# A selective scan rebuilt: one scan instruction for two states, decays in two places, D x as a matmul, B and C loaded in eight pieces

## What is computed

```python
x_inner, z = split(x @ W_in.T)
x_conv = silu(depthwise_causal_conv(x_inner, w_conv, b_conv))       # 4 taps
delta, Bm, Cm = split(x_conv @ W_x.T, [1024, 1040])
delta = softplus(delta @ W_dt.T + b_dt)
A = -exp(A_log)
decay = exp(d_t[..., None] * A)                                     # for each row t
state = decay * state + B_t[:, None, :] * x_t[..., None]            # 16 states a channel
y_t = einsum('bds,bs->bd', state, C_t) + x_t * D
out = (y * silu(z)) @ W_out.T                                       # added to x
```

## Time and profile before

| | us |
|---|---|
| median of 3 runs | 2681.13 (2676.42 to 2688.78) |
| the profiled execution, its time | 2680.24 |
| its span on the core | 2678.3 |
| first scan to last gate | 511.68 to 761.5 |
| busy in the whole span: TensorE, VectorE, ScalarE, GpSimd | 2498.9, 1819.6, 1121.8, 598.3 |

### The profile page before, as it was taken

The page is one execution under the profiler, slowest core; times in us unless marked ns, Lnnn a source line. Parts: engine busy times, 40 slices in busy tenths (PEclk is TensorE's granted clock), DMA queues, the critical chain, the costliest instruction groups (busy, mean ns, idle before and its releaser), DMA issues.

```text
span 2678.3 us, 33407 instructions
## 1 busy us (share of the span) xinstructions
PE 2498.9 (93%) x11618; PEld 1680.4 (63%) x11618; DVE 1819.6 (68%) x1995; ACT 1121.8 (42%) x1360; POOL 598.3 (22%) x420
## 2 busy tenths in 40 slices
PE   6999988887866999999999999999898899999998
PEld 5778767644333777777655555555486677777775
DVE  5878854388989577778875666666435766666665
ACT  2334422365444322222245555555333444555543
POOL 4555544388852311111200000000000000000000
PEclk9999999999977999999999999999898899999999
DMA  7677755622111233433332331332111366666563
GB/s 275 227 243 259 259 155 185 223 69 74 37 63 47 110 144 133 180 125 144 140 111 95 102 111 49 112 101 95 63 61 79 116 217 235 232 223 222 220 221 138
DMA packets 123660, 394.71 MB, mean 147 GB/s; under 512 B 23664, under 2 KB 39228, under 8 KB 97072
## 3 DMA queue, kind: packets, MB, share of 16 engines
q1 hardware_dynamic: 95584, 326.82, 34.5%
q10 hardware_dynamic: 27984, 66.66, 7.1%
HBM read 304.14 MB, written 89.30 MB: 147 GB/s over the span
## 4 chain that ended last, share of the span: by engine, by line
PE 72%; DVE 10%; DMA 9%; POOL 3%; ACT 3%; issue 2%; ACTq 1%; SPq 0%; DVEq 0%; POOLq 0%
PE ps L2079 16%; PE ps L2080 15%; PE ps L2081 15%; PE ps L2458 10%; PE ps L2468 9%; DMA w_halves<-unit_lo 7%; PE ps L2365 3%; DVE ps L1612 3%; POOL work L928 1%; PE ps L2719 1%; DVE work L1615 1%; DMA wT_lo<-w_halves 1%; DVE work L1612 1%; ACTq L1069 1%; DMA x_res<-in_x 1%
## 5 line engine op out<-in xcount | busy, mean ns | idle before, releaser
L1832 DVE TENSOR_TENSOR sums<-sums,pT 128x1024 f32<-128x1024 f32 x272 | 319.0, 1221 | 194.1 <-ACT pT L1313 192.8
L1770 DVE SCALAR_TENSOR_TENSOR peak<-ps,rs_all,peak 128x1024 f32<-128x1024 f32 x272 | 335.6, 1277 | 93.9 <-PE ps L2365 93.7
L1313 ACT ACTIVATE pT<-ps,rs_all 128x1024 f32<-128x1024 f32 x272 | 284.8, 1111 | 230.8 <-PE ps L2458 185.2
L2468 PE MATMUL ps<-pT,values 128*64 128x512 f32 x1088 | 256.4, 602 | 0.0
L2196 PE MATMUL ps<-work,ident 128*128 128x512 f32 x256 | 136.0, 632 | 41.2 <-POOL work L909 26.9
L978 POOL TENSOR_TENSOR cT_lo<-cT_raw,cT_hi 128x512 fp32r<-128x512 f32 x60 | 77.6, 1294 | 352.0 <-ACT cT_hi L1262 352.0
L2468 PEld LDWEIGHTS ps<-pT,values 128*64 128x64 f32 x1088 | 68.8, 136 | 132.9 <-issue 112.0
L1966 DVE TENSOR_TENSOR rgu_lo<-rgu_raw,rgu_hi 128x2048 fp32r<-128x2048 f32 x64 | 143.9, 2288 | 5.1 <-ACT rgu_hi L1396 5.1
L1612 DVE TENSOR_TENSOR_SCAN ps<-ps,work 128x512 f32<-128x512 f32 x97 | 118.3, 1220 | 23.7 <-ACT ps L1185 20.5
L872 POOL TENSOR_TENSOR ctx_lo<-ctx_raw,ctx_hi 128x512 fp32r<-128x512 f32 x64 | 104.3, 1629 | 131.4 <-DVE ctx_hi L1519 131.4
L1185 ACT ACTIVATE ps<-delta,a_neg 128x512 f32<-128x512 f32 x128 | 87.2, 689 | 96.5 <-DVE work L1615 86.6
(11 more groups left out here) (461 smaller groups left out, 6452.9 us busy)
## 6 DMA issues: line engine op xcount, KB each, us to landing
rgu_raw<-in_r_gate_up SPq DMA_DIRECT2D x64, 1024.0 KB, 4.8
rd_raw<-in_r_down SPq DMA_DIRECT2D x32, 1024.0 KB, 4.8
sh_raw<-in_s_parts SPq DMA_DIRECT2D x32, 768.0 KB, 4.3
key_rows<-key_hi SPq DMA_DIRECT2D x17, 1024.0 KB, 3.9
key_rows<-key_lo SPq DMA_DIRECT2D x17, 1024.0 KB, 5.9
value_rows<-values SPq DMA_DIRECT2D x17, 1024.0 KB, 8.9
ctxT_raw<-in_ctx_T SPq DMA_DIRECT2D x16, 1024.0 KB, 6.9
ctx_raw<-in_ctx SPq DMA_DIRECT2D x16, 1024.0 KB, 8.5
```

Source lines behind the costliest of these rows:

```text
L1313: nc.scalar.activation(pT[:, i], ps[:, b:b + 2], ACT.Exp, scale=rs_all[:, bass.ds(c * KT + attend_tile(j, i)[1], 1)]).then_inc(s4_exp.sem, 1)
L1770: nc.vector.scalar_tensor_tensor(peak[:, p], ps[:, b:b + 2], rs_all[:, bass.ds(c * KT + kt, 1)], peak[:, p], ALU.mult, ALU.max).then_inc(s ...
L1832: nc.vector.tensor_tensor(sums[:, p], sums[:, p], pT[:, i], ALU.add).then_inc(s4_sum.sem, 1)
L2468: done = nc.tensor.matmul(ps[e * DK:(e + 1) * DK, 6 + p], values[:, s, kt, h * DK:(h + 1) * DK], pT[:, i, e], start=start and kt == 0, sto ...
```

## The change

`far` steps become 14 whole steps: in these the product of both states is GpSimd's, in the other 50 it is VectorE's. One scan instruction runs over both states (1024 elements); so that nothing passes from one state to the next, the first element of each delta row is 1e22 and the rates are kept at or below -1e-20, which makes the first decay exp of at most -100. The decays get two places (banks 2, 3 and 6, 7), and ScalarE waits for step n - 2. D x is a row formed by ScalarE (`skip_part`) that TensorE adds to the sum; all blocks are summed in bank 0, gates come after step 8k. Relu of block 0 is VectorE's; a small Exp stands after the B and C loads. The sixteen rows of B and of C come in eight DMAs of 1 MB: four of the first half at wx blocks 1 to 4, four of the second after block 7; VectorE waits for the second half at step 4 alone. Six blocks of W_out get places of their own and are loaded after the last dt unit. Three of the four tiles of a block are projected at steps 38 to 41, 44, 52 and 60, the fourth tile (bank 2, a place of decays) at step 62 and behind the loop. `wkv_raw` is loaded when the projection is done, between the two halves of w_q.

```diff
-def far(n):
-    return n % 2 == 1 and n != STEPS - 1
+FAR_STEPS = (3, 8, 13, 18, 23, 28, 33, 37, 41, 45, 49, 53, 57, 60)
+def far(n):
+    return n in FAR_STEPS
+def decay_bank(n):
+    return 6 if n % 2 else 2
+OUT_BANK = (4, 5, 1, 2)
+FIRST_DECAY = 1e22
+LEAST_RATE = -1e-20
...
-PARTS_STEP = {1: 1, 2: 6, **{k: 11 + 4 * (k - 3) for k in range(3, IB)}}
+PARTS_STEP = {1: 1, 2: 5, **{k: 11 + 4 * (k - 3) for k in range(3, IB)}}
-GATES_STEP = {8: (3,), 35: (4, 5, 6, 7)}
+GATES_STEP = {8: (3,), 30: (4,), 33: (5, 6), 36: (7,)}
 def out_rows(n):
-    first = (LATE_PRODUCTS - LATE_AHEAD) // 2
-    if first <= n < first + IB:
-        return (n - first) // 2, (n - first) % 2
-    if n >= 5 * SGS + 4 and n % SGS in (4, 5):
-        return n // SGS - 1, n % SGS - 4
+    if 38 <= n < 42:
+        return n - 38
+    if n >= 5 * SGS + 4 and n % SGS == 4:
+        return n // SGS - 1
```

On SyncE:

```diff
+            sp.wait_ge(stream_mm, streamed("dt", IB - 1))
             for ib in range(IB):
-                if ib < 2:
-                    sp.wait_ge(stream_mm, STREAM_UNITS - 1 + ib)
-                else:
-                    sp.wait_ge(y_out, ib - 1)
-                load_halves(STREAM_UNITS + ib, ib % 2, wo_loaded[ib % 2])
-                if ib == 1:
-                    sp.dma_start(wkv_raw[:], a["L1_xattn_Wkv"].rearrange("(t p) n -> p t n", p=P)).then_inc(w4_loaded[1].sem, 16)
+                if ib == IB - 2:
+                    sp.wait_ge(stream_mm, STREAM_UNITS)
+                for half, halves in enumerate(out_weights(ib)):
+                    sp.dma_start(halves.bitcast(F32), split_dram[STREAM_UNITS + ib, half]).then_inc(wo_loaded[ib // (IB - 2)], 16)
...
             for w in range(2):
+                if w == 1:
+                    sp.wait_ge(s2_out, TT)
+                    sp.dma_start(wkv_raw[:], a["L1_xattn_Wkv"].rearrange("(t p) n -> p t n", p=P)).then_inc(w4_loaded[1].sem, 16)
                 for c in range(W_CHUNKS):
```

On GpSimd:

```diff
+            nc.gpsimd.memset(delta[:, :, 0:1], FIRST_DECAY).then_inc(first_decay, 1)
             def read_far(n):
-                pool.wait_ge(sc_scan, (n + 1) * SG)
-                nc.gpsimd.tensor_tensor(work[:, n % RING, SG - 1], work[:, n % RING, SG - 1], c_row(n % SGS * SG + SG - 1), ALU.mult).then_inc(sc_far, 1)
+                pool.wait_ge(sc_scan, n + 1)
+                nc.gpsimd.tensor_tensor(work[:, n % RING], work[:, n % RING], c_rows(n % SGS), ALU.mult).then_inc(sc_far, 1)
```

On ScalarE:

```diff
+            def load_bc(half, rows, r, k):
+                act_e.dma_start(rows[:, k, NS // 4 * r:NS // 4 * (r + 1)].rearrange("p s t -> p (s t)"),
+                                bc_parts[half, r, k].partition_broadcast(P)).then_inc(bc_loaded[half], 16)
             for ob in range(IB):
...
                 if ob == 1:
                     act_e.wait_ge(bc_stored, 16)
-                    load_bc(0, bc_first)
-            load_bc(1, bc_rest)
+                if 1 <= ob < 5:
+                    load_bc(0, bc_first, (ob - 1) // 2, (ob - 1) % 2)
+            for r in range(2):
+                for k in range(2):
+                    load_bc(1, bc_rest, r, k)
+            nc.scalar.activation(silu_warm[:], neg_half[:, 0:1], ACT.Exp)
...
+                nc.scalar.activation(delta[:, k, 1:T], ps[:, bank, 1:T], ACT.Abs, bias=b_dt[:, k:k + 1]).then_inc(dt_abs, 1)
                 if k:
                     act_e.wait_ge(dt_ready, k)
+                    nc.scalar.activation(bc_rows[:, 1:T], ps[:, bank, 1:T], ACT.Relu, bias=b_dt[:, k:k + 1]).then_inc(dt_relu, 1)
...
+            def skip_part(ib):
+                if ib:
+                    act_e.wait_ge(y_done, ib)
+                nc.scalar.activation(skip_row[:], x_conv[:, ib], ACT.Copy, scale=skip[:, ib:ib + 1]).then_inc(y_skip, 1)
...
+                if n >= 2 and far(n - 2):
+                    act_e.wait_ge(sc_scan, n - 1)
+                elif n >= 2:
+                    act_e.wait_ge(sc_read, near_steps(n - 2))
                 for e in range(SG):
-                    if n and e and far(n - 1):
-                        act_e.wait_ge(sc_scan, n * SG)
-                    elif n:
-                        act_e.wait_ge(sc_read, near_reads(n - 1, e))
-                    nc.scalar.activation(ps[:, DECAY_BANK + e], delta[:, ib], ACT.Exp, scale=a_neg[:, ib, g * SG + e:g * SG + e + 1]).then_inc(sc_decay, 1)
+                    nc.scalar.activation(ps[:, decay_bank(n) + e], delta[:, ib], ACT.Exp, scale=a_neg[:, ib, g * SG + e:g * SG + e + 1]).then_inc(sc_decay, 1)
+                if g == 4:
+                    skip_part(ib)
```

On VectorE:

```diff
-            nc.vector.tensor_scalar(a_neg[:], a_neg[:], -1.0, None, ALU.mult).then_inc(a_ready, 1)
+            nc.vector.tensor_scalar(a_neg[:], a_neg[:], -1.0, LEAST_RATE, ALU.mult, ALU.min).then_inc(a_ready, 1)
...
+            nc.vector.tensor_scalar(bc_rows[:, 1:T], ps[:, STREAM_BANK["dt", 0], 1:T], b_dt[:, 0:1], 0.0, ALU.add, ALU.max).then_inc(dt_relu, 1)
...
             def gate_rows(ib):
-                nc.vector.scalar_tensor_tensor(ps[:, ib % 2], x_conv[:, ib], skip[:, ib:ib + 1], ps[:, ib % 2], ALU.mult, ALU.add).then_inc(y_sum, 1)
-                nc.vector.tensor_tensor(x_conv[:, ib], ps[:, ib % 2], gate(ib), ALU.mult).then_inc(y_gate, 1)
+                nc.vector.tensor_tensor(x_conv[:, ib], ps[:, 0], gate(ib), ALU.mult).then_inc(y_gate, 1)
...
+                dve.wait_ge(sc_decay, (n + 1) * SG)
+                drive, state = flat(work[:, n % RING]), flat(ps[:, decay_bank(n):decay_bank(n) + SG])
+                nc.vector.tensor_tensor_scan(drive if far(n) else state, state, drive, 0.0, ALU.mult, ALU.add).then_inc(sc_scan, 1)
+                if not far(n):
+                    dve.wait_ge(sc_scan, n + 1)
+                    nc.vector.tensor_tensor(drive, state, flat(c_rows(g)), ALU.mult).then_inc(sc_read, 1)
+                if ib and g == 0:
+                    gate_rows(ib - 1)
```

On TensorE:

```diff
             def accumulate(n):
-                if g == 0 and ib >= 2:
-                    pe.wait_ge(y_gate, ib - 1)
+                if g == 0 and ib:
+                    pe.wait_ge(y_gate, ib)
...
                 for e in range(SG):
+                    done = nc.tensor.matmul(ps[:, 0], ident[:], work[:, n % RING, e], start=g == 0 and e == 0, stop=False)
                 done.then_inc(sc_y, 1)
+                if g == SGS - 1:
+                    pe.wait_ge(y_skip, ib + 1)
+                    nc.tensor.matmul(ps[:, 0], ident[:], skip_row[:], start=False, stop=True).then_inc(y_done, 1)
...
+                    for tt in range(TT - 1):
+                        project_rows(ib, tt)
+                if n == STEPS - 2:
+                    pe.wait_ge(sc_read, near_steps(n))
+                    for ib in range(3):
+                        project_rows(ib, TT - 1)
+            for ib in range(3, IB - 1):
+                project_rows(ib, TT - 1)
+            rows_loaded(IB - 1)
+            for tt in range(TT):
+                project_rows(IB - 1, tt)
```

More of the change, by code:

```diff
@@ L33, with near_steps, far_steps @@
 RING = 5
+FAR_STEPS = (3, 8, 13, 18, 23, 28, 33, 37, 41, 45, 49, 53, 57, 60)
 def far(n):
-    return n % 2 == 1 and n != STEPS - 1
-def near_reads(n, e):
-    return sum(SG - far(i) for i in range(n)) + e + 1
-def far_reads(n):
+    return n in FAR_STEPS
+def near_steps(n):
+    return sum(not far(i) for i in range(n + 1))
+def far_steps(n):
     return sum(far(i) for i in range(n + 1))
+def decay_bank(n):
[3 more added lines that the diff above has]
+LEAST_RATE = -1e-20
 EARLY_UNITS = ([("x", n, 0) for n in range(IB)] + [("z", n, 0) for n in range(3)] + [("bc", 0, h) for h in range(2)]
@@ L322, in b_rows, with out_weights, c_rows, flat @@
             return (bc_rest if half else bc_first)[:, 0, n:n + SG]
-        def c_row(n):
-            half, n = divmod(n, NS // 2)
-            return (bc_rest if half else bc_first)[:, 1, n]
+        def out_weights(ib):
+            if ib < IB - 2:
+                return wo_hi[:, ib], wo_lo[:, ib]
+            return tuple(half[:, ib - (IB - 2)].rearrange("p k i -> p (k i)") for half in (wT_hi, wT_lo))
+        def c_rows(g):
+            half, n = divmod(g * SG, NS // 2)
+            return (bc_rest if half else bc_first)[:, 1, n:n + SG]
+        def flat(rows):
+            return rows.rearrange("p b n -> p (b n)")
         s3 = Map(nc, base, 229344)
@@ L915, in add_soft @@
             def add_soft(k):
-                pool.wait_ge(dt_taken, 2 * (k + 1))
+                pool.wait_ge(dt_relu, k + 1)
                 pool.wait_ge(dt_l, k + 1)
-                nc.gpsimd.tensor_tensor(delta[:, k], bc_rows[:], delta[:, k], ALU.add).then_inc(dt_ready, 1)
+                nc.gpsimd.tensor_tensor(delta[:, k, 1:T], bc_rows[:, 1:T], delta[:, k, 1:T], ALU.add).then_inc(dt_ready, 1)
             for n in range(STEPS):
@@ L1605, in _ @@
+            dve.wait_ge(bc_loaded[0], 64)
             for n in range(STEPS):
                 ib, g = divmod(n, SGS)
+                if n == SGS // 2:
+                    dve.wait_ge(bc_loaded[1], 64)
```

(27 more changed lines are left out.)

97 lines of the change are left out of this document (41 added, 56 removed).

## The result

The changed kernel takes 2661.78 us (median of 7 runs, 2655.75 to 2665.54) against 2681.13 (7 runs, 2676.42 to 2688.78): ratio 0.9926, 95% interval [0.991, 0.9942]. The forecast was 2642 and its range ended at 2659: the direction was right, the size was not. 19.4 us were gained where 39 were expected. The profiled execution after has a span of 2659.6 us and TensorE's granted clock at 0.97.

The account below looks back on a forecast made before the run. VectorE was taken to set the scan's length (busy 224.5 of 249.8 us), GpSimd following closely. 2680.24 - 29.3 - 2.5 - 5.9 - 0.8 = 2641.7, with 0.9 for the median 2642 us; range 2630 to 2659.

Parts of the forecast that it names:

- Start of the scan and pieces: Ahead of the first scan: earlier decays and waiting only for bc_first, -2.5 us; eight-piece B and C loads end ScalarE's stall, -5.9.
- come back: Second-half B and C loads beside dt 1's weights: if they stall it as before, 3 to 6 us return.
- Scan stretch: First scan to last product: VectorE's own work 207.6 us plus waits 10.2 makes 217.8 against 247.1, -29.3 us.
- waits for decays and drives: VectorE's waits in the scan, 9.4 us forecast; the longest at steps 5 and 15, 2.8 us each.
- gate 2: Gate after far step 23, which reaches TensorE 2.4 + 1.1 + 0.6 us after its scan: 0.8 us of wait.
- Tail: End of the scan: D x matmul replaces L1598, -0.3; fourth-tile matmuls fill the gap, keeping TensorE's clock up, 0.5; sum -0.8 us.
- All else: Stages outside the scan's start, stretch and tail: no term in the sum, so no change.
- A: Rival: handovers eat half; each of seven periods waits a drive (2.3 us), or dt 1 comes late; 2658 us, chance 0.17.
- three signs of being wrong: Scan over 2.35 us; VectorE's longest waits for GpSimd's drives; stage after the scan starting with a wait for wkv_raw.
- B's stall: Rival: the DMA stall ahead of the scan stays despite the pieces; 2651 us, chance 0.12.
- C's stretching: Rival: GpSimd's instructions stretch 1.44 times beside VectorE's longer scans and GpSimd bounds; 2694 us, chance 0.03.
- D's cheaper scan: Rival: a scan of 1024 takes 1.75 us, VectorE has 34 us less, GpSimd bounds; 2627 us, chance 0.03.

Follow-up runs that it names:

- e7: Kernel before, with one part of the change alone: B and C loaded in eight pieces of four states; 2671.74 us, ratio 0.9983.
- e9: Changed kernel with B and C loaded in four pieces of eight states, as before the change; 2666.89 us, ratio 0.9963.
- e2: Changed kernel with TensorE's order at the scan's end altered: block 6 projected after step 59, fourth tiles moved; 2652.27 us, ratio 0.9886.
- e10: Changed kernel with each scan of 1024 elements issued as two of 512; 2657.53 us, ratio 0.9928.
- e13: The e4 kernel with far steps 9 and 22 in place of 8 and 23; 2645.74 us, ratio 0.9873.
- e12: Changed kernel with step 60's products on VectorE instead of GpSimd, TensorE's order as in the change; 2649.09 us, ratio 0.989.
- e4: Changed kernel with e2's order at the end and far steps 4, 14 in place of 3, 13; 2643.71 us, ratio 0.9874.
- e0: The kernel before, unchanged, measured and profiled again; 2677.79 us, ratio 0.9998.

## Why the prediction was wrong

The two profiled executions differ by 18.7 us where the sum had 38.5. The missing 19.8, by the steps of the sum:

1. **Start of the scan and pieces, -2.5 and -5.9: right.** The wx row is 5.7 shorter and the way from it to the first scan 2.3. TensorE's stall was the burst; e7 and e9 show it from both sides. What was hedged, that the stall of dt 1 may "come back", came in e2, e9, e10 and e13 with 2.9 to 4.8 us of waits at VectorE's second and third steps and is 0.4 us in the change's own profiles.
2. **Scan stretch, -29.3: it was -25.7 (3.6 missing).** Slots are 209.1 for 207.6, waits 12.3 for 10.2. The waits for decays and drives were right in sum (7.9 and 2.0 after the first scan for 9.4; step 24 took 1.3 for 0.3); the gates', 2.4 for 0.8, were not: I let only gate 2 be late, but gates 0, 3 and 4 also come before TensorE has the last sum and D x.
3. **Tail, -0.8: it was +5.5 (6.3 missing), the step that failed.** I worked it out from the last product on, as if TensorE were free then, and counted D x against L1598 and the fourth-tile matmuls against the gap. What I did not do was follow TensorE's own queue into that moment: a far step at 60, three steps from the end, makes it stand until GpSimd is through, at 721.45; nine matmuls of block 6 and nine of fourth tiles stand behind it, ahead of the sums. And a sum of a step is 1.88 us, not the 1.1 that stands in the prediction's working of gate 2: that was the row of one of a step's two matmuls. The trace before has 256 records for 128 of them:

```profile
L2196 PE MATMUL ps<-work,ident 128*128 128x512 f32 x256 | 136.0, 632 | 41.2 <-POOL work L909 26.9 <-DVE work L1615 14.2
```

   e12 shows that the wait goes when the stand and the clock behind it go; e2 and e4 show the same from the other side, since their order shortens the stand from 3.99 to 1.3 us.
4. **All else, no change: it was +9.5.** First stage 2.9, third stage 2.3, last attention stage 4.8, the rest -0.5. The prediction put this at nothing, and the scan's steps can't account for it; e0 has the third stage at 54.7 as well, and all three spread as much among builds of the changed kernel. With the misses of 1 to 3 alone, 10.3 us, the forecast of 2642 would have been 2652, inside its range. In the third stage VectorE's copy of col_max took 2.36 us for 0.42:

```profile
L1696 DVE COPY col_max<-h_abs x1: 2356/2356/2356, 763.7 to 763.7; 128x512 f32<-128x512 f32 x1
```

and GpSimd at that moment:

```profile
763.44 2.34 POOL L973 TENSOR_TENSOR wkv_lo<-wkv_raw,wkv_hi 128x1024 fp32r<-128x1024 f32 x1
```

The copy started 0.3 us behind it and ended 0.3 us after it. The Trainium skill (SBUF — State Buffer; Who interferes with whom) has it that a copy can enter a mode that takes the port pair shared with GpSimd, and that the later one then blocks for the whole instruction; the row agrees. In the kernel before the copy took 0.42 us, and GpSimd's instruction began 0.21 us behind it:

```profile
788.44 0.42 DVE L1660 COPY col_max<-h_abs 128x512 f32<-128x512 f32 x1
788.65 2.43 POOL L949 TENSOR_TENSOR wkv_lo<-wkv_raw,wkv_hi 128x1024 fp32r<-128x1024 f32 x1
```

In e0 the copy took 2.60, in e4 1.86, in e7 0.42: where GpSimd is in its row of wkv decides it. In the last attention stage TensorE does the same 428 matmuls at a lower granted clock. Cut from row_inv to rk, first before, then after, then e2_tail, where the stage took 111.4:

```profile
1892.74:2004.26 111.52, 99.73 (x428) 76.90 (x428) 47.63 (x57) 39.34 (x56) 6.32 (x10) 0.88 0.18 59
```

```profile
1869.84:1986.17 116.33, 104.54 (x428) 80.31 (x428) 47.65 (x57) 39.45 (x56) 6.32 (x10) 0.84 0.17 57
```

```profile
1870.67:1982.07 111.40, 99.60 (x428) 76.70 (x428) 47.64 (x57) 39.37 (x56) 6.33 (x10) 0.88 0.17 60
```

The 4.8 us of the stage are TensorE's 4.8 us. Over all sixteen profiles the length goes with the clock: 111.4 to 111.6 us at 0.88, 113.1 to 113.2 at 0.86, 113.7 to 114.6 at 0.85, 116.3 to 116.4 at 0.84. What sets the clock there, and what moves the first stage, no run shows.

By their own steps the three terms make -28.2 us of the change. The medians say -19.4 on the first chip and about -24 on the second. So 4 to 9 us of the loss elsewhere are in the medians too; which stretch holds them can't be read from one profile of each, and no run settles it.

Of the rivals, A named the right size (2658) by luck, for the wrong reason: it had each of seven periods wait 2.3 us for a drive, and there were two waits of 1.00. None of the three signs of being wrong that the prediction named came, since none of them looked at the last gate. B's stall went, C's stretching did not occur (2366 ns beside scans of 2.3 us), and D's cheaper scan neither.
